# Router logits from ten extra columns of the output projection, x times gate in its bias product, and seven dense experts ahead of the routed ones

## What is computed

```python
QKV = einsum('bsd,ed->bse', X, W_in) + b_in;  Q, K, V = split(QKV, 3)
Q, K = rope(Q, 128), rope(K, 128)
A = sum(K / max(norm(K), 1e-12) * V, axis=-2)          # one row of 256
x = layernorm(2 * X + einsum('bsd,ed->bse', A * Q, W_out) + b_out)
probs = softmax(x @ gate_w)                              # 8 experts
gate_score, gate_idx = top_k(probs, 2); gate_score /= sum(gate_score)
combine = (gate_score on its experts) * alpha
y_e = gelu(x @ fc1_w[e] + fc1_b[e]) @ fc2_w[e] + fc2_b[e]
out = layernorm(x + sum_e combine[:, e] * y_e)
```

## Time and profile before

| | |
|---|---|
| runs | 123.48, 123.06, 122.69 us; median 123.06 |
| the profiled execution | 122.73 us, of which the span of the trace is 120.8 us |
| busy PE / DVE / ACT / POOL | 107.9 / 72.9 / 57.3 / 60.2 us |
| mean granted TensorE clock | 0.985 of full speed |
| DMA, mean over the span | 210 GB/s |

### The profile page before, as it was taken

The page is one execution under the profiler, slowest core; times in us unless marked ns, Lnnn a source line. Parts: engine busy times, 40 slices in busy tenths (PEclk is TensorE's granted clock), DMA queues, the critical chain, the costliest instruction groups (busy, mean ns, idle before and its releaser), DMA issues.

```text
span 120.8 us, 2383 instructions
## 1 busy us (share of the span) xinstructions
PE 107.9 (89%) x701; PEld 96.1 (80%) x701; DVE 72.9 (60%) x207; ACT 57.3 (47%) x150; POOL 60.2 (50%) x94
## 2 busy tenths in 40 slices
PE   6779999899799998899799899999999999997900
PEld 6768888888679996879569799999999999985700
DVE  0287877869964738895161756566644554526770
ACT  4434896752552664532303663645444423532480
POOL 7905899708700001085878889805465456302200
PEclk9999999999999999999999999999999999999985
DMA  2899999999994220073235677664776722259425
GB/s 91 270 288 407 416 426 359 348 349 347 383 396 160 91 87 0 0 218 137 87 90 163 195 213 216 214 204 114 240 218 239 227 76 87 92 131 345 175 100 204
DMA packets 14984, 25.36 MB, mean 210 GB/s; under 512 B 1651, under 2 KB 7964, under 8 KB 14588
## 3 DMA queue, kind: packets, MB, share of 16 engines
q1 hardware_dynamic: 13676, 21.68, 53.0%
...
...
## 4 chain that ended last, share of the span: by engine, by line
PE 47%; DMA 13%; DVE 11%; POOL 10%; issue 5%; SPq 5%; ACT 4%; ACTq 0%; DVEq 0%; POOLq 0%
PE ps L1319 16%; PE ps L1331 15%; DMA wq<-in_w_q_t 5%; DMA gT_lo<-pair_rows 4%; PE ps L1157 3%; PE ps L1300 3%; POOL x L441 2%; DMA gT_hi<-x_rows,gather_i 2%; PE ps L1089 2%; POOL x L442 2%; DMA pair_rows<-kv,scatter_i 2%; SPq L347 2%; PE ps L1081 2%; POOL kv L445 2%; ACT z L714 2%
## 5 line engine op out<-in xcount | busy, mean ns | idle before, releaser
L671 ACT ACTIVATE g<-ps,cols 128x128 f32<-128x128 f32 x42 | 13.1, 363 | 23.0 <-issue 12.7
L1319 PEld LDWEIGHTS ps<-early,rT 128*128 128x128 f32 x168 | 21.9, 191 | 1.3 <-DVE early L975 0.3
L1319 PE MATMUL ps<-early,rT 128*128 (+1 forms) x168 | 22.2, 275 | 0.0
L1331 PE MATMUL ps<-wres,g 128*128 x84 | 21.7, 381 | 0.5 <-issue 0.5
L470 POOL DMA_INDIRECT pair_rows<-kv,scatter_i x13 | 12.6, 970 | 13.4 <-DVE kv L1020 13.1
L1013 DVE TENSOR_TENSOR y_plus<-ps,b_all 128x256 f32<-128x256 f32 x21 | 8.9, 424 | 12.3 <-PE ps L1331 11.9
L1331 PEld LDWEIGHTS ps<-wres,g 128*128 128x128 f32 x84 | 14.3, 191 | 1.8 <-issue 0.7
L1020 DVE SCALAR_TENSOR_TENSOR kv<-y_plus,w_step,kv 128x256 f32 x21 | 10.2, 485 | 2.8
L463 POOL DMA_INDIRECT gT_hi<-x_rows,gather_i x8 | 8.0, 1001 | 2.6 <-issue 1.7
L1210 PE MATMUL ps<-x0T,wres 128*128 128x128 f32 x64 | 8.5, 279 | 0.0
L1089 PE MATMUL ps<-ones 128*128 128x128 f32 x44 | 7.5, 333 | 1.0 <-POOL ones L405 1.0
...
## 6 DMA issues: line engine op xcount, KB each, us to landing
...
```

Of the source, the lines that this page charges most:

```text
L671: a.activation(g[:, s % 2, m, :], two(H_BANK, s)[:, tile(m)], ACT.Gelu, bias=b1_flat[:, m:m + KD * (E - 1) + 1][:, bass.ds(b1_at[s], 1)]). ...
L1319: last = nc.tensor.matmul(two(H_BANK, s)[:, tile(m)], w1_now[:, s % W1_SLOTS, k, tile(m)], x[:, tile(k)], start=k == 0, stop=k == KD - 1)
L1331: last = nc.tensor.matmul(two(Y_BANK, s), g[:, s % 2, k, :], weights(KD + k, s), start=k == 0, stop=k == KD - 1)
```

## The change

The logits no longer wait for the first norm. With a gate matrix whose column means are taken off (`gate_w`, made from `gw` on the chip), the logits of x1 are those of `z` times 1/std, and the order of a token's logits doesn't depend on that factor. So `z` gets ten more columns (`z_gate`, `acc_gate`, 266 wide): eight logits, minus the mean, and one of zeros. They come out of the output projection, whose weights get ten more columns: `w_out_n` times `gate_w`, taken once on PE. The part of x in them, x times gate, is computed by `x_gate` (stationary `gate_stat`, 84 columns, moving the parts of x transposed), split by ACT and DVE into `out_stat` (rows 64 to 83 high, 96 to 115 low), and enters through the bias product, whose stationary is now `out_stat` (128 rows, 128 columns of it for each tile) and whose moving side has twice the identity in those rows. The routing starts from `z_gate` directly; the gap of the two best logits is multiplied with 1/std later.

Further: for tiles 4 to 7 the variance comes from a sum of squares on ACT (`square_sum`), and POOL writes their x1. Only tile 0 is still transposed (x0T). All `x1_transpose`, `gate` and the `stay_warm` of that stretch go. `cols` is loaded earlier and is larger (116 columns for 50), `bo` is 128 by 266 for 33 by 256, `w_out_n` is one more load of 256 KB. The bias split (`bo_parts`) moves behind the rotation of K on POOL. `DENSE_BEHIND` is 1: expert 6 is computed ahead of the routed loop.

```diff
-DENSE_BEHIND = 2
+DENSE_BEHIND = 1
...
+GATE_COLS = 10
+X_HIGH, X_LOW = 64, 96
...
-        DENSE_LAST = (E - 1, E - 2)
+        DENSE_LAST = (E - 1,)
...
+            sp.dma_start(cols[:], columns).then_inc(l_cols, 16)
             sp.dma_start(bo[:], b_out).then_inc(l_bo, 16)
             sp.dma_start(rtok[:], rope_tok).then_inc(l_rtok, 16)
             sp.dma_start(wq[:], w_q_t).then_inc(l_wq, 16)
-            sp.dma_start(acc[:], x_tok).then_inc(l_x, 16)
-            sp.dma_start(cols[:], columns).then_inc(l_cols, 16)
+            sp.dma_start(acc, x_tok).then_inc(l_x, 16)
             sp.dma_start(rT[:], rope_t).then_inc(l_rT, 16)
-            sp.dma_start(wout[:], w_out_t).then_inc(l_wout, 16)
-            sp.dma_start(b2[:], fc2_b).then_inc(l_b2, 16)
+            sp.dma_start(wout[:, :, 0:D], w_out_t).then_inc(l_wout, 16)
+            sp.dma_start(w_out_n_sb, w_out_n).then_inc(l_wout, 16)
+            sp.dma_start(b2[:], fc2_b).then_inc(l_exp, 16)
...
-                    sp.wait_ge(x1_last_ok, 2)
+                    sp.wait_ge(x1_pool_ok, 2 * j + 2 - T // 2)
...
+            for j in range(T // 4, T // 2):
+                pool.wait_ge(shift_ok, j + 1)
+                for t in (2 * j, 2 * j + 1):
+                    g_.tensor_scalar(x1[:, t, :], z[:, t, :], rstd[:, t:t + 1], shift[:, t:t + 1],
+                                     ALU.mult, ALU.add).then_inc(x1_pool_ok, 1)
...
-            act.wait_ge(l_wout, 16)
+            act.wait_ge(l_wout, 32)
+            act.wait_ge(w_gate_ok, 1)
...
+            def x_gate_high(n):
+
+                act.wait_ge(x_gate_mm, n + 1)
+                a.copy(out_stat[X_HIGH:X_HIGH + 2 * G, half(n)],
+                       ps[X_HIGH:X_HIGH + 2 * G, X_GATE_BANK[n], :]).then_inc(x_gate_hi_ok, 1)
+
             q_raw()
+            act.wait_ge(pad_ok, 5)
+            x_gate_high(0)
             q_pass(1)
+            x_gate_high(1)
             q_rot_high(1)
 
...
+            def square_sum(t):
+
+                act.wait_ge(z_ok, t + 1)
+                a.activation(x1[:, t, :], z[:, t, :], ACT.Square, bias=z_gate[:, t, D + E:D + E + 1],
+                             accum_out=sq_sum[:, t:t + 1]).then_inc(sq_ok, 1)
+
+            def root_of_sum(j):
+
+                act.wait_ge(sq_ok, 2 * j + 2 - T // 2)
+                a.activation(sd[:, 2 * j:2 * j + 2], sq_sum[:, 2 * j:2 * j + 2], ACT.Sqrt, scale=1.0 / D,
+                             bias=eps[:]).then_inc(sd_ok, 1)
+
             root(0)
             normalise(0, z, x1, shift_ok, x1_ok)
             root(1)
-            x1_across(0)
+            square_sum(4)
+            square_sum(5)
+            root_of_sum(2)
+            act.wait_ge(x0T_mm, 1)
+            a.copy(x0T[:], ps[:, X0T_BANK, 0:D].rearrange("p (k c) -> p k c", k=KD)).then_inc(x0T_ok, 1)
             normalise(1, z, x1, shift_ok, x1_ok)
-            root(2)
-            x1_across(2)
-            normalise(2, z, x1, shift_ok, x1_ok)
-            root(3)
-
-            x1_across(4)
-            a.copy(x0T[:], x1T[:, 0, :, :]).then_inc(x0T_ok, 1)
-            x1_across(6)
+            square_sum(6)
+            square_sum(7)
+            root_of_sum(3)
             a.activation(table_unused[:, 0:1], eps[:], ACT.Gelu)
...
+            dve.wait_ge(l_cols, 16)
+            dve.wait_ge(gate_sum_mm, 1)
+            v.tensor_copy(mean_w[:], ps[:, GATE_W_BANK, SUM_AT:SUM_AT + E]).then_inc(gate_w_ok, 1)
+            dve.wait_ge(gate_w_ok, 1)
+            v.scalar_tensor_tensor(out=gate_w[:, :, 0:E], in0=mean_w[:].unsqueeze(1).to_broadcast([P, KD, E]),
+                                   scalar=-1.0 / D, in1=gw, op0=ALU.mult, op1=ALU.add).then_inc(gate_w_ok, 1)
+            dve.wait_ge(gate_w_ok, 2)
+            dve.wait_ge(pad_ok, 5)
+            v.tensor_copy(gate_stat[:, :, X_HIGH:X_HIGH + G], gate_w[:]).then_inc(gate_w_ok, 1)
             kv_out(4)
+            dve.wait_ge(gate_w_ok, 3)
+            v.tensor_tensor(gate_stat[:, :, X_HIGH + G:], gate_w[:], raw(gate_stat[:, :, X_HIGH:X_HIGH + G]),
+                            ALU.subtract).then_inc(gate_w_ok, 1)
             dve.wait_ge(wq_hi_ok, 1)
             v.tensor_tensor(wq_lo[:], wq[:], raw(wq_hi[:]), ALU.subtract).then_inc(wq_lo_ok, 1)
             kv_out(5)
...
+            dve.wait_ge(w_gate_mm, 1)
+            v.tensor_copy(wout[:, :, D:D + G],
+                          ps[:, GATE_W_BANK, W_GATE_AT:W_GATE_AT + KD * G].rearrange("p (k g) -> p k g", k=KD))\
+             .then_inc(w_gate_ok, 1)
...
+
+            def x_gate_low(n):
+
+                dve.wait_ge(x_gate_hi_ok, n + 1)
+                v.tensor_tensor(out_stat[X_LOW:X_LOW + 2 * G, half(n)], ps[X_HIGH:X_HIGH + 2 * G, X_GATE_BANK[n], :],
+                                raw(out_stat[X_HIGH:X_HIGH + 2 * G, half(n)]), ALU.subtract).then_inc(x_gate_lo_ok, 1)
+
+            dve.wait_ge(bo_ok, 2)
+            v.tensor_copy(bo_parts[0:OUT_LOW + 1, D:D + G], ps[0:OUT_LOW + 1, GATE_W_BANK, B_GATE_AT:B_GATE_AT + G])\
+             .then_inc(w_gate_ok, 1)
+            dve.wait_ge(w_gate_ok, 2)
+            v.tensor_tensor(bo_parts[OUT_LOW:OUT_LOW + 1, D:D + G],
+                            ps[OUT_LOW:OUT_LOW + 1, GATE_W_BANK, B_GATE_AT:B_GATE_AT + G],
+                            raw(bo_parts[OUT_LOW:OUT_LOW + 1, D:D + G]), ALU.subtract).then_inc(w_gate_ok, 1)
+            x_gate_low(0)
             q_pass_low(1)
+            x_gate_low(1)
...
+            def scales_of_sum(j):
+
+                two = slice(2 * j, 2 * j + 2)
+                dve.wait_ge(sd_ok, j + 1)
+                v.reciprocal(rstd[:, two], sd[:, two]).then_inc(rstd_ok, 1)
+                dve.wait_ge(rstd_ok, j + 1)
+                v.tensor_tensor(shift[:, two], z_gate[:, two, D + E], rstd[:, two], ALU.mult).then_inc(shift_ok, 1)
...
             first_stats(1)
             first_sum(2)
             norm_scales(1, sd_ok, rstd_ok, shift_ok)
-            x1_across(1)
-            first_stats(2)
             first_sum(3)
-            x1_across(3)
...
-            normalise_last(z, x1, sd_ok, rstd_ok, x1_last_ok)
-            x1_across(5)
-            x1_across(7)
-
+            scales_of_sum(2)
...
-            lg = ps[:, LG_BANK, 0:T * E].rearrange("p (t e) -> p t e", t=T)
+            lg = z_gate[:, :, D:D + E]
             place = ps[:, POS_BANK, 0:RT * E]
             begins = ps[:, POS_BANK, RT * E + 1:(RT + 1) * E]
-            dve.wait_ge(lg_mm, T)
+            dve.wait_ge(z_ok, T)
...
             largest(1, lg2[:])
+            scales_of_sum(3)
             dve.wait_ge(all_ones_ok, 2)
             v.tensor_tensor(chosen[:, 0:RT, :], sel[:, 0, routed, :], sel[:, 1, routed, :], ALU.add).then_inc(chosen_ok, 1)
+            step(v.tensor_tensor(gap[:], top[:, 0, :], top[:, 1, :], ALU.subtract))
+            dve.wait_ge(rstd_ok, T // 2)
+            v.tensor_tensor(gap[:], gap[:], rstd[:], ALU.mult).then_inc(gap_ok, 1)
             step(v.tensor_reduce(chosen_sum[:], sel[:, :, routed, :].rearrange("p k t e -> p e k t"),
...
             x_evict(0)
             x_evict(1)
             dense_add(5)
+            dense_add(6)
             dense_add(DENSE_AHEAD)
...
             dense_add(DENSE_AHEAD + 1)
-            dense_add(DENSE_AHEAD + 2)
...
+                if t == 2:
+                    pe.wait_ge(l_cols, 16)
+                    for k in range(KD):
+                        last = nc.tensor.matmul(ps[:, GATE_W_BANK, SUM_AT:SUM_AT + E], raw(ones[:]), gw[:, k, :],
+                                                start=k == 0, stop=k == KD - 1)
+                    last.then_inc(gate_sum_mm, 1)
...
+            pe.wait_ge(l_wout, 32)
+            pe.wait_ge(gate_w_ok, 2)
+            pe.wait_ge(pad_ok, 2)
+            for k in range(KD):
+                nc.tensor.matmul(ps[0:OUT_LOW + 1, GATE_W_BANK, B_GATE_AT:B_GATE_AT + G], b_out_two[:, k, :], gate_w[:, k, :],
+                                 start=k == 0, stop=k == KD - 1)
+            for m in range(KD):
+                for k in range(KD):
+                    last = nc.tensor.matmul(ps[:, GATE_W_BANK, W_GATE_AT + m * G:W_GATE_AT + (m + 1) * G],
+                                            w_out_n_sb[:, k, tile(m)], gate_w[:, k, :], start=k == 0, stop=k == KD - 1)
+            last.then_inc(w_gate_mm, 1)
...
+            def x_gate(n):
+
+                for k in range(KD):
+                    for part in (fT_hi, fT_lo):
+                        last = nc.tensor.matmul(ps[0:X_HIGH + 2 * G, X_GATE_BANK[n], :], gate_stat[:, k, :],
+                                                part[:, k, half(n)], start=k == 0 and part is fT_hi,
+                                                stop=k == KD - 1 and part is fT_lo)
+                last.then_inc(x_gate_mm, 1)
+
             q_block(1, 0)
+            pe.wait_ge(gate_w_ok, 4)
+            pe.wait_ge(acol_ok, KD)
+            x_gate(0)
             q_block(1, 1)
...
+            x_gate(1)
 
             def out_bias(t):
```

(42 more changed lines are left out.)

134 lines of the change are left out of this document (49 added, 85 removed).

## The result

The changed kernel takes 121.94 us in the median of 20 runs; beside them the kernel before took 124.2 us (20 runs). The ratio of the two is 0.989, 95% interval 0.986 to 0.992: 1.1% faster, about 1.4 us. Against the 123.06 us from which the forecast started that is 121.7 us. The forecast was 121.1 us, 1.6% faster. So the direction and the range held, and the gain is two thirds of what was forecast.

A forecast was written before the change was run, and what follows sets the result against it. It took attention to gate, then DVE's routing and gathers, then PE's routed loop and DMA as bounding. Gathers 4.15 us earlier less 2.25 for the seventh expert gave 1.9 off 123.06: 121.15, stated as 121.1 us, range 119.8 to 123.0.

The forecast's parts named there:

- Small matmuls, 1.7 us: PE ahead of the projection: the column sum, `w_gate` and the bias part add rows costing 0.42 + 1.25 = 1.7 us.
- The relay: DVE's steps ahead of the projection, awaited by the bias products: first product at 31.7 us, 3.5 us later than before.
- the first rival: Handovers ahead of the projection and the tanh come 0.7 and 0.5 us later still: 122.3 us, chance 0.10.
- No gap around 128 rows: In the projection, starts around the bias product become 0.12 us apart, saving 0.38 us a tile.
- the second rival: In the projection, the bias costs what it did, four tiles 0.38 us longer: +1.2, 122.3 us, chance 0.10.
- Routing +0.95: Inside the routing, added steps cost 0.65 us and a wait for ACT's tanh 0.3; `gather_i` still 4.15 us earlier.
- Seventh expert +2.25: Ahead of the routed loop, dense expert 6 on PE delays the first routed matmul by 2.25 us.
- The loop keeps its pace: The routed loop runs at the same pace as before, so its earlier start of 1.9 us carries through.
- the rival of the freer loop: Gathers and weights lead the routed loop by 2 us more, removing 0.45 us of first-step waits: 119.8 us, chance 0.10.
- the end is DMA: Behind the routed loop, DMA sets the end, which stays the same from last scatter to store.
- The clock rival: PE idles from about 41.1 to 43.5 us, its clock halves ahead of the gathers: 125.6 us, chance 0.07.
- The bounds: Relay +0.7, seventh expert -0.85 to +0.65, POOL and ACT together +0.7, each alone: 120.3 to 122.4 us.

The follow-up runs named there:

- bias128: The kernel before, with only the projection's bias operands changed to 128 rows (126 of them zeros) instead of 33: 1.1% faster, interval 0.983 to 0.996, median 121.50 us.
- six_ahead: The changed kernel with six dense experts ahead of the routed loop and two behind it, so the gate part alone: ratio 0.970 to the kernel before.
- old start: Group name for kernels without the gate part: the kernel before and variants of it; no time of its own.
- changed start: Group name for kernels with the gate part: the changed kernel and variants of it; no time of its own.
- old_seven: The kernel before, with seven dense experts ahead of the routed loop and one behind: ratio 1.013, median 124.76 us.

## Why the prediction was right in direction and too large

By its own steps, with the two profiles of the changed kernel:

- *Small matmuls, 1.7 us.* The rows of `w_gate` and the bias part (L1195, L1199) put the feature sum 1.23 us further behind the last product of Q, and the column sum took 0.36: 1.6 in all, right.
- *The relay: first product at 31.7.* 32.18 and 31.31; the first execution had its K/V stage 0.95 us behind the second by variation. Set against the stage's start in the old profile (7.52), both give 31.7. Right, and the first rival fell.
- *No gap around 128 rows.* Right, and shown alone by `bias128`; the second rival fell. The rule of the Trainium skill, "TensorE: Matmul & The Clock Gate", section "LDWEIGHTS (loading the stationary operand)", by which the time of a weight load doesn't go by the rows, agrees with the trace: the load of 33 rows took 0.183 us and that of 128 rows 0.188. What the 33 rows cost is something else. An ordinary load starts 0.12 us ahead of its own matmul, beside the one before; the load of the 33 rows and the next one start together with their matmuls (33.28 and 33.59), so nothing hides them, and the three starts take 0.38 us more. The prediction wrongly took the rule as speaking against the gap. Why the loads don't start early there, no run shows.
- *Last z 39.15, routing 39.5.* 39.51 and 38.60; 39.70 and 38.79. Right.
- *Routing +0.95, gather_i 50.7, second gather 56.0.* 50.86; 56.05 and 55.19. The tanh was done at 44.11, where 44.3 was set. POOL's two-scalar step took 0.588 us for 128x256, under my lower bound of 0.7.
- *Seventh expert +2.25.* 2.56 by the earlier trace rows against the changed profile, 2.44 against `six_ahead`: right, and 0.2 to 0.3 too small. Worth nothing behind the loop: right.
- *First routed matmul 60.4.* 60.71 and 59.85. Right.
- *"The loop keeps its pace"*: the pace yes, 1.76 us a step, but the loop took 40.46 us, not 41.20. One early stall of 0.48 us is missing, as the rival of the freer loop has it; but it is missing in `bias128` too, where the loop has no more lead, so this is luck and not that rival. Last scatter 2.3 and 3.2 us earlier, more than the 1.9 forecast.
- *"and the end is DMA", "the same end from scatter to store"*: **this is the step that failed.** The prediction took the end as a constant of 17.3 us. It was 19.1 and 20.7. Behind the last pair nothing changed (6.9 us to the end, 6.9 and 7.1 after); the difference lies in the reload. Last scatter to last pair took 10.4 to 11.8 us in the three profiles of the old start, and 11.7 to 12.9 in those of the changed start whose issue was held and whose clock stayed: about 1.2 us more, 0.6 to 1.4 of them in the issues themselves. Counted from the reload's first issue, it is 8.0 to 8.7 against 9.3 to 10.5. Where the clock fell in the wait, last scatter to last pair took 12.9 to 15.8. The profile from which the 17.3 was read had the shortest end of the three, so a part of the difference is luck too: `old_seven` has 17.8 and `bias128` 18.7.
- *The clock rival* had its place and its direction right and its size wrong: it happens in a part of the executions, lasts 3.4 us where the prediction needed 6.2 for it to decide, and costs 0.7 us ahead of the gathers. The fall that costs more is at the end, where I had not looked: behind the last scatter PE is idle for over 2 us in one piece.
- *The bounds.* "Each alone" gives at most 121.15 + 0.7 = 121.85 us; the 122.4 that was written takes two of them together.

So the mechanism up to the loop was right, and the sum took 1.9 us at the start of the loop for the gain of the kernel, where the end gives 1 us or more back. That the forecast lies as near as it does is in part luck: the last scatter came 0.4 to 1.3 us sooner than it said.
